# Stage 0 of a windowed-attention block: a new order of work at its front seams

## The reference

```
idx = jnp.arange(seq_len)
mask = jnp.abs(idx[:, None] - idx[None, :]) <= 16       # 16 tokens to either side
mask = mask.at[0, :].set(True); mask = mask.at[:, 0].set(True)   # token 0 is global
q, k, v = proj(Wq), proj(Wk), proj(Wv)                   # (B, 16, S, 8)
scores = jnp.where(mask, q @ k.T * 8 ** -0.5, -inf)
out = (softmax(scores) @ v) @ Wo.T

def ternary_quantize(w):                                 # used by blocks 2 and 4
    delta = 0.7 * jnp.mean(jnp.abs(w))
    return where(w > delta, 1.0, where(w < -delta, -1.0, 0.0))
```

## Time and profile before

| what | us |
|---|---|
| median of 3 runs | 1157.03 |
| profiled execution, its own time | 1156.63 |
| its span (first to last instruction) | 1154.9 |
| stage 0, to the end of the last windowed unit | 212.7 |
| TensorE busy / VectorE busy over the span | 1001.4 / 834.3 |

### The profile page before, as it was taken

The page is one execution under the profiler, slowest core; times in us unless marked ns, Lnnn a source line. Parts: engine busy times, 40 slices in busy tenths (PEclk is TensorE's granted clock), DMA queues, the critical chain, the costliest instruction groups (busy, mean ns, idle before and its releaser), DMA issues.

```text
span 1154.9 us, 32337 instructions
## 1 busy us (share of the span) xinstructions
PE 1001.4 (87%) x13347; PEld 464.4 (40%) x13347; DVE 834.3 (72%) x1039; ACT 750.2 (65%) x1497; POOL 132.2 (11%) x416
## 2 busy tenths in 40 slices
PE   4798999775486999999999899999989998999964
PEld 1444545432242244344443443434434444444433
DVE  4453655254664999999879789977878997799512
ACT  2511545358332499999676789866768987699921
POOL 8100111000000000000102020010212001010000
PEclk8787999878777999999999899988989999899975
DMA  3663342200008223311000025200004420010000
GB/s 100 174 191 67 90 102 75 56 1 1 0 1 262 44 49 72 70 33 28 12 11 15 22 84 127 66 12 12 14 20 123 102 54 12 11 46 17 20 16 18
DMA packets 60386, 64.47 MB, mean 56 GB/s; under 512 B 17424, under 2 KB 39184, under 8 KB 60112
## 3 DMA queue, kind: packets, MB, share of 16 engines
q1 hardware_dynamic: 60240, 62.40, 20.5%
HBM read 27.06 MB, written 35.32 MB: 54 GB/s over the span
## 4 chain that ended last, share of the span: by engine, by line
DVE 48%; PE 35%; issue 5%; DMA 5%; ACT 4%; SPq 2%; POOL 0%; POOLq 0%; ACTq 0%; DVEq 0%
DVE nmf L1582 39%; PE wide L658 22%; PE bank L658 13%; DVE xcsq L1371 1%; DVE xp L1371 1%; DMA KQs<-mw_dram 1%; ACT xcsq L1132 1%; DMA x<-xT 1%; DMA mw_dram<-nmt 1%; ACT big L1132 1%; DVE xcsq L1380 1%; DVE big L1740 1%; SPq L366 1%; ACT L1132 1%; SPq L433 1%
## 5 line engine op out<-in xcount | busy, mean ns | idle before, releaser
L1582 DVE TENSOR_REDUCE nmf<-wide 128x1 f32<-128x1024 f32 x512 | 589.9, 1207 | 50.5 <-PE wide L658 50.0
L1132 ACT ACTIVATE big<-wide 128x512 f32<-128x512 f32 x684 | 392.0, 601 | 94.4 <-PE wide L658 82.7
L658 PE MATMUL wide<-big,KQs 48*128 48x512 bf16 (+1 forms) x1376 | 358.6, 350 | 5.7 <-DVE nmf L1582 4.4
L658 PE MATMUL bank<-big,V 128*9 128x128 f32 x8192 | 328.2, 279 | 11.6
L658 PE MATMUL wide<-KQs,big 50*128 50x512 bf16 (+1 forms) x1036 | 273.6, 330 | 5.7 <-ACT big L1132 5.7
L658 PEld LDWEIGHTS bank<-big,V 128*9 128x9 f32 x8192 | 178.4, 91 | 239.0 <-ACT big L1132 194.9
L1132 ACT ACTIVATE big<-bank 128x512 f32<-128x512 f32 (+1 forms) x468 | 232.1, 515 | 45.9 <-PE bank L658 40.2
L658 PE MATMUL bank<-KQs,big 50*128 50x512 bf16 x340 | 132.7, 390 | 4.3 <-ACT big L1132 4.3
L658 PEld LDWEIGHTS wide<-KQs,big 50*128 50x128 bf16 x1036 | 70.7, 95 | 114.9 <-ACT big L1132 57.5
L1132 ACT ACTIVATE scr<-wide 128x380 f32<-128x380 f32 (+3 forms) x128 | 61.1, 485 | 84.6 <-PE wide L658 73.8
L1534 DVE TENSOR_REDUCE nmw<-wide 95x4 f32<-95x512 f32 (+1 forms) x96 | 61.2, 640 | 60.1 <-PE wide L658 59.0
(11 more groups left out here) (212 smaller groups left out, 812.8 us busy)
## 6 DMA issues: line engine op xcount, KB each, us to landing
o_dram<-big SPq DMA_DIRECT2D x128, 64.0 KB
big<-kf_dram SPq DMA_DIRECT2D x32, 200.0 KB
kf_dram<-scr SPq DMA_DIRECT2D x24, 256.0 KB, 3.1
qf_dram<-scr SPq DMA_DIRECT2D x24, 256.0 KB, 3.9
KQs<-qf_dram SPq DMA_DIRECT2D x32, 192.0 KB
ow_dram<-scr SPq DMA_DIRECT2D x32, 142.5 KB
big<-kw_dram SPq DMA_DIRECT2D x16, 275.0 KB
kw_dram<-scr SPq DMA_DIRECT2D x12, 352.0 KB, 5.5
```

Source lines behind the costliest of these rows:

```text
L658: return nc.tensor.matmul(o, l, r, start=start, stop=stop, **kw)
L1132: return nc.scalar.activation(o, i, f, **kw)
L1582: nc.vector.tensor_reduce(nmf[:, i % 4, c:c + 1], wide[:, k:k + 2, :].rearrange("p g c -> p (g c)"), AX.X, ALU.max, negate=True).then_inc( ...
```

## The change

The first projections of TensorE no longer wait for the key windows. The wait moves in front of each batch's first key chunk and counts per batch. The key windows are copied by three instructions per batch instead of eleven, of batch 0 first and of batch 1 ahead of VectorE's work on the first value chunk of batch 0. The ternary and bias chain leaves the seam between the projections and the windowed attention: TensorE's two small products go behind `values(7)` in unit 8, VectorE's parts behind maxima of units 11, 13 and 16, and TensorE's wait for them in front of `values(8)`. `zero_divide` keeps its ten instructions but does its two readings of bank 7 first; `values(1)` waits for those two alone, `zero_column` runs at u == 4, `zero_out` after the first maximum of unit 10 and behind `pv_evac` 4, and `values(5)` waits for it. The results in bank 6 stand in columns 400 and 408 in place of 0 and 8, since `values` writes columns 0 to 284.

```diff
@@ -182,7 +182,7 @@
         w_sum, w_scaled, w_centred = sem("w_sum"), sem("w_scaled"), sem("w_centred")
         b_mean, b_centred, b_sum = sem("b_mean"), sem("b_centred"), sem("b_sum")
         mt_mm, mt_evac, mt_add, mt_spread = sem("mt_mm"), sem("mt_evac"), sem("mt_add"), sem("mt_spread")
-        win_ready = sem("win_ready")
+        win_first, win_ready = sem("win_first"), sem("win_ready")
         proj_mm = sem("proj_mm")
         part1, residue = sem("part1"), sem("residue")
         part2, part3, part_v = sem("part2"), sem("part3"), sem("part_v")
@@ -719,12 +719,12 @@
 
             def ternary():
                 pe.wait_ge(tw, 1)
-                mm(bk(6)[:, 8:10], meanw[:, :], bias[:, BI["ld_b"]:BI["ld_b"] + 2]).then_inc(b_mean, 1)
-                mm(bk(6)[:, 0:1], ones[:, :], ts_[:, 0:1]).then_inc(tw_sum, 1)
+                pe.wait_ge(pv_evac, 7)
+                mm(bk(6)[:, 408:410], meanw[:, :], bias[:, BI["ld_b"]:BI["ld_b"] + 2]).then_inc(b_mean, 1)
+                mm(bk(6)[:, 400:401], ones[:, :], ts_[:, 0:1]).then_inc(tw_sum, 1)
 
             def project_window():
                 pe.wait_ge(xn_ready, NC)
-                pe.wait_ge(win_ready, 3)
                 free = []
                 m = 0
                 for n, (kind, b, mov, cols, at) in enumerate(chunks()):
@@ -734,6 +734,9 @@
                             pe.wait_ge(part_v, count)
                         else:
                             pe.wait_ge(residue, count)
+                    if kind == "k" and at == 0:
+                        pe.wait_ge(win_first, b + 1)
+                        pe.wait_ge(win_ready, b + 1)
                     wn = w("w%s0" % kind)
                     if kind == "v":
                         for t in range(at, at + cols // P):
@@ -810,8 +813,6 @@
                 pe.wait_ge(part3, QK_W)
                 pe.wait_ge(part_v, CHUNKS_W - QK_W)
                 pe.wait_ge(win_const, 1)
-                pe.wait_ge(tw, 2)
-                pe.wait_ge(b_sum, 1)
                 keep_busy(2, bk(6))
                 keep_busy(20, bk(7))
 
@@ -860,7 +861,12 @@
                     if u == 0:
                         pe.wait_ge(g0v, 4)
                     if u == 1:
+                        pe.wait_ge(g0v, 6)
+                    if u == 5:
                         pe.wait_ge(g0v, 15)
+                    if u == 8:
+                        pe.wait_ge(tw, 2)
+                        pe.wait_ge(b_sum, 1)
                     if u >= 2:
                         pe.wait_ge(pv_evac, u - 1)
                     for j in range(3):
@@ -888,7 +894,7 @@
                 zero_values()
                 for u in range(UNITS):
                     ahead = u + AHEAD_W < UNITS
-                    if u == 1:
+                    if u == 4:
                         zero_column()
                     if u % 6 == 3:
                         pe.wait_ge(pv_evac, u - 1)
@@ -903,6 +909,8 @@
                                 maximum(u + AHEAD_W, g, y)
                         if g == 1 and u:
                             values(u - 1)
+                        if g == 1 and u == 8:
+                            ternary()
                 values(UNITS - 1)
 
             def spread_means():
@@ -1112,7 +1120,6 @@
                 if stage == 0:
                     pe.wait_ge(w_loaded, 48)
                     project_window()
-                    ternary()
                     windowed_attention()
                     project_out_window()
                 if stage in (1, 3):
@@ -1170,7 +1177,7 @@
                 act.wait_ge(xn_ready, NC)
                 for b in range(B):
                     act.copy(xwin[:, b, :, P - 1:P],
-                             xp[:, b, HALF:HALF + 1].unsqueeze(1).broadcast_to((P, WT, 1))).then_inc(win_ready, 1)
+                             xp[:, b, HALF:HALF + 1].unsqueeze(1).broadcast_to((P, WT, 1))).then_inc(win_first, 1)
 
                 def second(m, r, o):
                     act.wait_ge(residue, m + 1)
@@ -1405,18 +1412,21 @@
 
             def centre_biases():
                 dve.wait_ge(b_mean, 1)
-                m = bk(6)[:, 8:10]
+                dve.wait_ge(tw_sum, 1)
+                m = bk(6)[:, 408:410]
                 nc.vector.tensor_reduce(bmean[:, :], m, AX.X, ALU.add)
                 b = bias[:, BI["ld_b"]:BI["ld_b"] + 2]
                 tt(b, b, m, ALU.subtract).then_inc(b_centred, 1)
                 dve.wait_ge(b_centred, 1)
-                tt(bmean[:, :], bmean[:, :], bk(6)[:, 9:10], ALU.add).then_inc(b_sum, 1)
-
-            def ternary():
+                tt(bmean[:, :], bmean[:, :], bk(6)[:, 409:410], ALU.add).then_inc(b_sum, 1)
+
+            def ternary_sum():
                 nc.vector.tensor_reduce(ts_[:, 0:1], w("tern"), AX.X, ALU.add,
                                         apply_absolute_value=True).then_inc(tw, 1)
+
+            def ternary():
                 dve.wait_ge(tw_sum, 1)
-                nc.vector.tensor_scalar(ts_[:, 1:2], bk(6)[:, 0:1], 1.0 / (P * P), 0.7,
+                nc.vector.tensor_scalar(ts_[:, 1:2], bk(6)[:, 400:401], 1.0 / (P * P), 0.7,
                                         ALU.mult, ALU.mult).then_inc(tw, 1)
                 dve.wait_ge(tw, 2)
                 nc.vector.tensor_scalar(ts_[:, 2:3], ts_[:, 1:2], -1.0, None, ALU.mult).then_inc(tw, 1)
@@ -1428,11 +1438,15 @@
                 tt(tern[:, :], tg[:, 0, :], tg[:, 1, :], ALU.subtract).then_inc(tw, 1)
 
             def project_window():
-                for b in range(B):
-                    dve.wait_ge(xn_ready, NC)
-                    for t in range(WT):
-                        ins = nc.vector.tensor_copy(xwin[:, b, t, 0:P - 1], xp[:, b, QT * t:QT * t + P - 1])
-                ins.then_inc(win_ready, 1)
+                def windows(b):
+                    over = P - 1 - QT
+                    nc.vector.tensor_copy(xwin[:, b, :, 0:QT], xp[:, b, 0:QW].rearrange("p (t k) -> p t k", k=QT))
+                    nc.vector.tensor_copy(xwin[:, b, 0:WT - 1, QT:P - 1],
+                                          xp[:, b, QT:QW].rearrange("p (t k) -> p t k", k=QT)[:, :, 0:over])
+                    nc.vector.tensor_copy(xwin[:, b, WT - 1, QT:P - 1], xp[:, b, QW:QW + over]).then_inc(win_ready, 1)
+
+                dve.wait_ge(xn_ready, NC)
+                windows(0)
 
                 def third(m, r, o):
                     dve.wait_ge(part2, m + 1)
@@ -1441,6 +1455,8 @@
                 before = None
                 m = 0
                 for n, (kind, b, _, cols, at) in enumerate(chunks()):
+                    if kind == "v" and b == 0 and at == 0:
+                        windows(1)
                     if kind != "v":
                         o, r = (partk if kind == "k" else partq)[:, :, at:at + cols], res[:, m % CBUF, 0:cols]
                         dve.wait_ge(part1, m + 1)
@@ -1500,25 +1516,27 @@
 
             def zero_divide():
                 dve.wait_ge(g0, 4)
-                k = 4
+                k = 6
                 for b in range(B):
                     tt(o0[:, b, :, :], bk(7)[0:H, 160 * b:160 * b + H * (D + 1)].rearrange("p (h d) -> p h d", h=H),
                        hmaskT[:, :, :], ALU.mult).then_inc(g0v, 1)
-                    dve.wait_ge(g0v, k + 1)
+                dve.wait_ge(g0v, 6)
+                for b in range(B):
                     nc.vector.tensor_reduce(o0s[:, b, :], o0[:, b, :, :].rearrange("p h d -> p d h"), AX.X,
                                             ALU.add).then_inc(g0v, 1)
+                    dve.wait_ge(g0v, k + 1)
+                    nc.vector.reciprocal(s0s[:, b, 2:3], o0s[:, b, D:D + 1]).then_inc(g0v, 1)
                     dve.wait_ge(g0v, k + 2)
-                    nc.vector.reciprocal(s0s[:, b, 2:3], o0s[:, b, D:D + 1]).then_inc(g0v, 1)
-                    dve.wait_ge(g0v, k + 3)
                     nc.vector.tensor_scalar(o0s[:, b, 0:D], o0s[:, b, 0:D], s0s[:, b, 2:3], None,
                                             ALU.mult).then_inc(g0v, 1)
-                    dve.wait_ge(g0v, k + 4)
+                    dve.wait_ge(g0v, k + 3)
                     tt(z0[:, b, :, :], hmaskT[:, :, 0:D], o0s[:, b, 0:D].unsqueeze(1).broadcast_to((H, H, D)),
                        ALU.mult).then_inc(g0v, 1)
-                    k += 5
+                    k += 4
 
             def zero_out():
                 dve.wait_ge(g0, 5)
+                dve.wait_ge(pv_evac, 4)
                 nc.vector.tensor_copy(q0o[:, :], bk(7)[:, 400:400 + B]).then_inc(g0v, 1)
 
             def turn(j, s):
@@ -1544,8 +1562,15 @@
                         maximum(u, g)
                         if g == 0 and u:
                             turn(u - 1, u - 1)
-                        if u == AHEAD_W + 1 and g == 0:
+                        if u == AHEAD_W + 5 and g == 0:
                             zero_out()
+                        if u == AHEAD_W + 6 and g == 1:
+                            ternary_sum()
```

(8 more changed lines are left out.)

## The result

The changed kernel has a median of 1137.47 us over 6 runs (1135.06 to 1144.26), the kernel before 1157.07 over 6 (1148.64 to 1159.32) on the same chip. The ratio is 0.9857, 95% interval 0.9816 to 0.9899: 1.4% or 16.5 us less, against 15.3 forecast. The profiled execution is the slowest of the six, 1144.26 us with a span of 1142.4, so its trace shows 12.5 us of gain and not the 19.6 between the medians.

A forecast was written before the change was run, and what follows sets the result against it. Three seams were taken to lie alone on the chain of waits, mostly VectorE's and TensorE's: 5.0 + 1.9 + 8.8 - 0.4 = 15.3 us off 1156.6, forecast 1141.7 us from the median. Range 1136 to 1145, with cold and queue rivals 1134 to 1151.

The forecast's parts named there:

- Seam 1: First projections: TensorE starts at 22.8 in place of 28.32, 5.5 us, less 0.5 lost; 5.0 us carried.
- 0.5 was lost at the key stores: Batch 1's copies delay the third part of batch 0's last key chunk 0.6 past SyncE; 0.5 us taken as lost.
- the middle of two bounds: Time of a batch's three window copies on VectorE: 0.7 us if all fixed cost, 2.7 at most; 1.7 taken.
- Seam 2: Ternary and bias chain between last projection and fillers: fillers wait only for the last value copy; 1.9 us go.
- The cover: Units 6 to 14: chain is SyncE's and the queue's, hiding TensorE's 0.7 us of products; cost 0, or 1.5 without it.
- Seam 3: Query 0, unit 1 to the fillers at u == 3: no wait for `z`, clock stays up; 18.5 us become 9.7, gain 8.8.
- The new wait: Second unit: TensorE waits for unit 6's first maxima, queued behind `zero_divide` on VectorE; 1.0 us given back.
- the first rival: Clock falls all the same near unit 1; seam 3 gives only 4.3 us, 10.8 in all, 1146.2; chance 0.22.
- the cold band: Fillers at u == 3 fail to raise the clock, units 3 to 8 stay cold; 3.4 us lost, 1160.4; chance 0.05.
- The wait for the queue: Rival: a load of maxima for unit 6 comes late behind operand group 4; 5.9 us in all, 1147.6; chance 0.13.
- The copies were the cause: Denies the rival that something else held TensorE at 28.3; seam 1's 5.0 would go, 1146.7 left; chance 0.04.

The follow-up runs named there:

- late_copies: The changed kernel with batch 1's three copies moved behind the third part of batch 0's last key chunk; 1137.44 us in a single run.
- combined2: The changed kernel with groups 4 to 7 on ScalarE's queue, prologue fillers, `zero_divide` cut in two, batch 1's copies later, `centre_weights` at unit 21; 1135.35 us, ratio 0.9814.
- wait_filled: The kernel before with 16 filler matmuls on TensorE in front of its wait for `z` at u = 1; 1150.13 us, ratio 0.9964.
- s3_query0: The kernel before with only the query 0 edits: `zero_divide` reordered, `zero_column` at u = 4, `zero_out` in unit 10; 1146.78 us, ratio 0.992.
- warm_prologue: The changed kernel with 4 fillers before and 3 behind `zero_turn` in the prologue; 1137.29 us, ratio 0.9862.
- combined: The changed kernel with the prologue's fillers, batch 1's operand groups issued in halves, and `zero_divide` cut in two; 1140.57 us, ratio 0.9862.
- s1_eleven: The kernel before with only the first projections' order changed, keeping eleven copies per batch; 1151.12 us, ratio 0.9953.

## Why the prediction was right

**Size and sign.** The median, 1137.47, lies 4.2 us below the forecast of 1141.7 and in the range. The sum of the forecast's steps in the profile is closer than that: 5.2 + 1.8 + 9.1 - 0.5 = 15.6 against 15.3. The steps are right one by one; that the whole is as near is in part luck. The profile also has terms that the forecast lacked (below), its span is only 12.5 us shorter, and the 19.6 us between the medians cannot be traced to steps at all.

**Seam 1** (5.0 forecast, 5.2 measured at the landing). TensorE started 5.7 us earlier and 0.5 was lost at the key stores, as sized. The size of that loss is not confirmed: the six profiles with this order land 5.0 to 5.9 us earlier than before, and the two without the copies there (`late_copies`, `combined2`) 5.9 and 6.0. The timeline of the changed kernel, VectorE:

```profile
34.34 1.23 DVE L1443 COPY xcsq<-xp 128x1045 f32<-128x1045 f32 x1
35.49 0.31 DVE L1444 COPY xcsq<-xp 128x320 f32<-128x320 f32 x1
35.73 0.17 DVE L1446 COPY xcsq<-xp 128x32 f32<-128x32 f32 x1
```

The three copies take 1.6 us (34.34 to 35.90), near the 1.7 taken as the middle of two bounds. By the Trainium skill's rule that the prediction cites ("VectorE: DVE Perf Modes", "What auto-detection actually checks") they would have taken an estimated 0.73 us and their fixed parts; the 1045 elements took 1.23 us, 0.85 an ns, so the measurement goes against it for the large copy, while the 320 took 0.31 us, 1.03 an ns with the fixed part in.

**Seam 2** (1.9 forecast, 1.8 measured). The fillers follow the last value copy. VectorE's wait for TensorE's products was 0.53 us (0.5 put) and its work 1.6 (116.92 to 118.55):

```profile
116.92 0.16 DVE L1417 TENSOR_REDUCE bmean<-bank 128x1 f32<-128x2 f32 x1 [0.53 <-PE bank L658]
...
118.26 0.29 DVE L1378 TENSOR_TENSOR tern<-tg 128x128 f32<-128x128 f32 x1
```

One step failed in a small way. I took TensorE's products as hidden because the chain would be SyncE's between units 6 and 14. After the change it is TensorE's until 128.27: the row `115.66 1.14 ... x26` is `values(7)` with the four products, 0.5 us longer than a plain `values`, on the chain. The cover was itself a function of the lateness that the change removed.

**Seam 3** (8.8 forecast, 9.1 measured). The new wait is 0.7 us (1.0 forecast), the units and fillers run at the high clock, `zero_column` costs 0.53 at u == 4 (0.4 forecast). `wait_filled` shows the split between wait and clock, 3.2 and 5.9, where the expectation of `s3_query0` had 3.6 and 5.2.

**The rivals.** The clock did not fall near unit 1 in the changed kernel nor in `s3_query0`, so the first rival and the cold band did not occur in any profile here. The wait for the queue did not move ahead of unit 14 and did not grow. That a faster front lengthens that wait is not shown: it was 3.2 in `s3_query0` and 3.6 in `wait_filled`, but 2.4 in the changed kernel and 2.1 in `warm_prologue`, which reach it earlier; the 5.7 us of `combined` came with halved groups. The copies were the cause: the order alone brings the gain (`s1_eleven`).

**What the forecast lacked.** Two clock effects, which nearly cancel in the profile by luck: the fillers ahead of the windowed units ran at the high clock from the start (+2.6 us; the forecast had put up to 3 in its range, not in its sum), and the prologue lost 3.0 to a stretch at the low one. Behind the fillers at u == 3 another 2.2 went, mainly 0.5 + 0.5 for the two small steps and a low stretch of 6.8 us in place of 3.4 behind the wait at unit 14. The faster fillers go with seam 2; the low stretches differ between kernels that do the same in those places. From the last windowed unit to the end, where no kernel of the study changes anything, the profiles take 935.6 (`s3_query0`) to 943.5 us (`combined2`), 942.2 before and 943.2 after. A spread of 8 us without an edit is half of the effect measured.

## What to carry to other kernels

Ahead of a filler or a well-fed stretch, price a wait of TensorE by its idle time and by what runs at the low clock behind it: here 3.2 and 5.9 us. When small work is moved out of a seam into a steady loop, ask what is queued behind it on its engine; whether a longer chain elsewhere covers it must be judged for the kernel as it will be. Once several waits in series are removed, the next fixed transfer may take part of the gain back (here 3.3 us in `combined`, nothing in `warm_prologue`), so check one that is nearly critical before adding up further gains.

## What was not expected of the hardware

- The clock fell in the changed kernel's prologue at about 72.9 although TensorE had waited only 0.5 us, up to 72.54; what it ran next was 22 transposes of 16 columns. In three kernels the stretch differed with the same instructions: 10.2 us low in the changed kernel, 3.4 before and 6.8 in `late_copies`, and in these two it began only after the transposes. With seven filler matmuls around them it stayed at 1.00 in all three profiles.
- A 4 KB load issued beside four transfers of 196 to 275 KB took 6.9 to 7.7 us to land on the same queue, 5.4 behind half of them, and 6.8 and 7.8 with the large ones on another engine's queue.
- One 128x1045 copy took 1.23 us and a 128x320 one 0.31 on the same engine: the first moves 0.85 elements an ns, the second 1.03 with its fixed part included.
